# Adding the causal mask of the plain scores on VectorE, inside the maximum's instruction, instead of with a mask matmul

## What is computed

```python
score = jnp.einsum('bhqd,bhkd->bhqk', Q, K) / scale
causal = jnp.tril(jnp.ones((1, 1, seq, seq), dtype=jnp.float32))
score = score - 10000000000.0 * (1.0 - causal)
score = score - jnp.max(score, axis=-1, keepdims=True)
weights = jax.nn.softmax(score, axis=-1)
attn = jnp.einsum('bhqk,bhkd->bhqd', weights, V)
```

## Time and profile before

| | us |
|---|---|
| median of 3 runs | 498.72 |
| lowest, highest | 497.11, 499.74 |
| span of the profiled execution | 495.2 |
| busy: PE / PEld / DVE | 463.4 / 296.0 / 323.8 |
| busy: ACT / POOL | 285.1 / 166.9 |

### The profile page before, as it was taken

One profiled execution on the slowest core, in us unless ns is written; L12 is line 12 of the kernel. 1 busy time (PEld: TensorE's weight loads), 2 busy tenths in 40 slices (PEclk: granted clock), 3 DMA queues, 4 the chain that ended last, 5 costly groups with the idle time before them and its releaser, 6 DMA issues.

```text
span 495.2 us, 10480 instructions
## 1 busy us (share of the span) xinstructions
PE 463.4 (94%) x2676; PEld 296.0 (60%) x2676; DVE 323.8 (65%) x802; ACT 285.1 (58%) x594; POOL 166.9 (34%) x167
## 2 busy tenths in 40 slices
PE   5779999999999999999999999989999999999992
PEld 2346555555554654655655545447887787787781
DVE  3879757777677676777776774313656756756743
ACT  1311146765766766767657666956565565565560
POOL 4524010230411402402304112126645564564661
PEclk9986579999999999999999999999999999999997
DMA  7877411212112112202121000000000000000000
GB/s 249 267 226 192 122 21 26 68 33 66 40 19 64 40 19 64 57 18 67 37 65 39 3 1 3 2 0 1 1 1 3 21 0 0 21 0 0 22 0 22
DMA packets 41738, 23.49 MB, mean 47 GB/s; under 512 B 31280, under 2 KB 33968, under 8 KB 41712
## 3 DMA queue, kind: packets, MB, share of 16 engines
q1 hardware_dynamic: 41712, 23.18, 17.1%
HBM read 14.26 MB, written 8.65 MB: 46 GB/s over the span
## 4 chain that ended last, share of the span: by engine, by line
PE 77%; DVE 7%; issue 4%; ACT 4%; DMA 4%; SPq 3%; POOL 1%; DVEq 0%; ACTq 0%; POOLq 0%
PE bank L960 20%; PE bank L975 15%; PE bank L1044 14%; PE bank L938 14%; PE bank L1055 7%; DVE maxima L703 2%; PE bank L993 2%; DMA k_scratch<-rope_lo 2%; PE bank L941 2%; ACT num L600 1%; DVE num L763 1%; DVE num L836 1%; ACT num L539 1%; SPq L314 1%; PE bank L1020 1%
## 5 line engine op out<-in xcount | busy, mean ns | idle before, releaser
L539 ACT ACTIVATE num<-bank 128x512 f32<-128x512 f32 (+3 forms) x384 | 168.8, 495 | 101.6 <-PE bank L960 99.1
L703 DVE TENSOR_REDUCE maxima<-bank 128x1 f32<-128x512 f32 (+15 forms) x384 | 182.3, 519 | 66.9 <-PE bank L941 46.2
L960 PE MATMUL bank<-q_op,k_op 128*128 128x512 f32 (+3 forms) x384 | 148.2, 419 | 2.8 <-ACT num L539 1.7
L938 PE MATMUL bank<-k_op,q_op 128*128 128x512 f32 (+15 forms) x384 | 126.3, 369 | 3.4 <-issue 2.9
L437 POOL TENSOR_SCALAR_AFFINE_SELECT num<-num 128x512 f32<-128x512 f32 x64 | 40.6, 635 | 226.0 <-ACT num L539 224.1
L960 PEld LDWEIGHTS bank<-q_op,k_op 128*128 128x128 f32 x384 | 71.4, 197 | 69.1 <-ACT num L539 62.0
L468 POOL TENSOR_TENSOR q_op<-num,q_op 128x512 fp32r<-128x512 f32 x64 | 82.4, 1290 | 63.6 <-ACT q_op L593 60.3
L938 PEld LDWEIGHTS bank<-k_op,q_op 128*128 128x128 f32 x384 | 77.0, 202 | 19.2 <-DVE maxima L703 10.9
L1044 PE MATMUL bank<-q_op,w_hi 128*128 (+1 forms) x256 | 81.9, 401 | 1.7 <-DVE num L836 1.6
L975 PE MATMUL bank<-num,v_op 128*32 128x512 f32 (+3 forms) x768 | 82.5, 503 | 0.0
L836 DVE TENSOR_TENSOR num<-bank,num 128x512 f32<-128x512 f32 x64 | 44.2, 691 | 58.5 <-ACT num L600 54.8
(11 more groups left out here) (86 smaller groups left out, 315.7 us busy)
## 6 DMA issues: line engine op xcount, KB each, us to landing
k_op<-k_scratch SPq DMA_DIRECT2D x16, 256.0 KB, 2.7
q_op<-q_scratch SPq DMA_DIRECT2D x64, 52.0 KB
w_raw<-in_w_all SPq DMA_DIRECT2D x6, 512.0 KB, 4.3
q_scratch<-rope_hi SPq DMA_DIRECT2D x8, 256.0 KB, 3.1
k_scratch<-rope_hi SPq DMA_DIRECT2D x8, 256.0 KB, 3.6
xT<-in_x_feat SPq DMA_DIRECT2D x4, 256.0 KB, 6.1
k_scratch<-k_op SPq DMA_DIRECT2D x2, 512.0 KB, 6.2
q_scratch<-rope_lo SPq DMA_DIRECT2D x4, 256.0 KB, 3.9
```

The lines of the kernel that those rows point to most:

```text
L539: act.activation(num[:, t % PB, h, off:CH], t_bank[k % TB][:, off:CH], ACT.Exp, scale=scale)\
L703: dve.tensor_reduce(maxima[:, half, j:j + 1], s_bank[k % SB][:, 0:width], AX.X, ALU.max)\
L938: ins = pe.matmul(s_bank[k % SB][:, 0:width], q_op[u][:, j, :, :].rearrange("p h q -> p (h q)"), k_op[u][:, lo:lo + width], start=True, st ...
L960: pe.matmul(t_bank[k % TB][:, off:CH].rearrange("p (j q) -> p j q", q=QD), k_op[w][:, kt * P:(kt + 1) * P], q_op[w][:, c * NB + off // QD: ...
```

## The change

The mask matmul at L941 goes; every plain unit is one matmul. The mask tile becomes `causal`, 512 columns wide in the tile `resid`: DVE clears the first 480 columns at the start of the program, and SP, after waiting for that, loads the 32 columns of the mask behind them, in fp32. For a diagonal unit DVE issues `tensor_tensor_reduce`, which adds the unit's last `width` columns of `causal` to the scores, writes the sum to one of three SBUF tiles (nothing reads them) and takes the maximum. Units that are not diagonal keep `tensor_reduce`. Ahead of the new instruction stands `dve.sem_inc(dve_turn, 1)`. In the first unit DVE also waits for the mask's load. The bf16 copies, their two casts on ScalarE and PE's wait for them go.

```diff
@@ -33,6 +33,7 @@
 QROWS = 3 * DH + 2
 KROWS = 3 * DH
 MASKED = -1e30
+LOWEST = -3e38
 FT = F // P
 UNITS = E * FT
 
@@ -177,8 +178,6 @@
 
         cos_sb, sin_sb = sb("cos_sb", [P, S]), sb("sin_sb", [P, S])
         ident = sb("ident", [P, P])
-        mask_f = sb("mask_f", [P, QD])
-        ident_b, mask_b = sb("ident_b", [P, P], BF16), sb("mask_b", [P, QD], BF16)
         tri = sb("tri", [P, 2, E * E])
         wqk = sb("wqk", [P, 4, D])
         wv, wo = sb("wv", [P, D]), sb("wo", [P, D])
@@ -210,6 +209,7 @@
 
         mg_w, mg_t, x1_w, x1_tw = (sb(n, [P, CH]) for n in ("mg_w", "mg_t", "x1_w", "x1_tw"))
         resid = sb("resid", [P, CH])
+        causal, masked_s = resid, (mg_w, mg_t, x1_w)
         x1 = xT[:, :].rearrange("p (t d) -> p t d", d=D)
 
         flat = [q_op[u][:, :, :, :].rearrange("p j h q -> p (j h q)") for u in range(2)]
@@ -248,7 +248,7 @@
         max_split, small_ready, small_read = sem("max_split"), sem("small_ready"), sem("small_read")
         rows_loaded = [sem(f"rows_loaded{c}") for c in range(NC)]
         dve_step, dve_turn, pool_turn = sem("dve_step"), sem("dve_turn"), sem("pool_turn")
-        w_split, w_hi_done, small_cast = sem("w_split"), sem("w_hi_done"), sem("small_cast")
+        w_split, w_hi_done, causal_cleared = sem("w_split"), sem("w_hi_done"), sem("causal_cleared")
 
         c_mg, c_mgt, c_mgs, c_y, c_var, c_rstd, c_x1, c_x1t, c_hi, c_log, c_lo, c_tanh, c_store, c_top = (
             sem(n) for n in ("c_mg", "c_mgt", "c_mgs", "c_y", "c_var", "c_rstd", "c_x1", "c_x1t",
@@ -277,7 +277,8 @@
                     sp.dma_start(sin_sb[:, cols], sin_t[:, cols]).then_inc(ld_tab[ch], 16)
                 if ch == 0:
                     sp.dma_start(wv[:, :], vw).then_inc(ld_v, 16)
-            for dst, src in ((ident[:, :], ident_d), (mask_f[:, :], mask_d)):
+            sp.wait_ge(causal_cleared, 1)
+            for dst, src in ((ident[:, :], ident_d), (causal[:, CH - QD:CH], mask_d)):
                 sp.dma_start(dst, src).then_inc(ld_small, 16)
 
             sp.wait_ge(ops_filled, 1)
@@ -504,10 +505,6 @@
                                bank[3][:, :], ACT.Copy).then_inc(v_copied, 1)
 
             for n in range(2 * CHUNKS):
-                if n == 4:
-                    act.wait_ge(ld_small, 16 * 2)
-                    act.activation(ident_b[:, :], ident[:, :], ACT.Copy).then_inc(small_cast, 1)
-                    act.activation(mask_b[:, :], mask_f[:, :], ACT.Copy).then_inc(small_cast, 1)
                 if n in (PROJ_FIRST - 1, PROJ_FIRST + 1):
                     copy_v((n - PROJ_FIRST + 1) // 2)
                 act.wait_ge(roped_ready, n + 1)
@@ -642,6 +639,7 @@
             dve.sem_inc(f_lo, HB)
 
 
+            dve.memset(causal[:, 0:CH - QD], 0.0).then_inc(causal_cleared, 1)
             for u in range(2):
                 dve.memset(v_op[u][:, :, :, :], 0.0).then_inc(v_cleared, 1)
             dve.wait_ge(v_cleared, 2)
@@ -700,8 +698,16 @@
                         lo = half * CH
                         width = min(CH, QD * (j + 1) - lo)
                         dve.wait_ge(s_ready, NS * s + k + 1)
-                        dve.tensor_reduce(maxima[:, half, j:j + 1], s_bank[k % SB][:, 0:width], AX.X, ALU.max)\
-                            .then_inc(s_reduced, 1)
+                        if QD * (j + 1) - lo <= CH:
+                            if k == 0 and plan is PROLOGUE:
+                                dve.wait_ge(ld_small, 16 * 2)
+                            dve.sem_inc(dve_turn, 1)
+                            dve.tensor_tensor_reduce(masked_s[k % SB][:, 0:width], s_bank[k % SB][:, 0:width],
+                                                     causal[:, CH - width:CH], 1.0, LOWEST, ALU.add, ALU.max,
+                                                     maxima[:, half, j:j + 1]).then_inc(s_reduced, 1)
+                        else:
+                            dve.tensor_reduce(maxima[:, half, j:j + 1], s_bank[k % SB][:, 0:width], AX.X, ALU.max)\
+                                .then_inc(s_reduced, 1)
                         done += 1
                         if done == SEG_S[0]:
                             split_max(s, 0, chain)
@@ -910,7 +916,6 @@
                 if n == PROJ_FIRST - 2:
                     project_v(0)
             pe.wait_ge(ld_small, 16 * 2)
-            pe.wait_ge(small_cast, 2)
             pe.sem_inc(pv_done, PB)
 
             def stage(plan, s, u, turn_u, turn_v, small):
@@ -933,14 +938,9 @@
                         once(k_loaded[u][half], turn_u * 16, ("k", half))
                         lo = half * CH
                         width = min(CH, QD * (j + 1) - lo)
-                        diagonal = QD * (j + 1) - lo <= CH
                         pe.wait_ge(s_reduced, NS * s + k + 1)
-                        ins = pe.matmul(s_bank[k % SB][:, 0:width], q_op[u][:, j, :, :].rearrange("p h q -> p (h q)"),
-                                        k_op[u][:, lo:lo + width], start=True, stop=not diagonal)
-                        if diagonal:
-                            ins = pe.matmul(s_bank[k % SB][:, width - QD:width], ident_b[:, :], mask_b[:, :],
-                                            start=False, stop=True)
-                        ins.then_inc(s_ready, 1)
+                        pe.matmul(s_bank[k % SB][:, 0:width], q_op[u][:, j, :, :].rearrange("p h q -> p (h q)"),
+                                  k_op[u][:, lo:lo + width], start=True, stop=True).then_inc(s_ready, 1)
                     if step[0] == "P":
                         if step[1] + 1 < 2 * CHUNKS:
                             project(step[1] + 1)
```

## The result

| | before | after |
|---|---|---|
| median of the runs, us | 498.69 (497.11 to 499.74, 4 runs) | 503.56 (501.81 to 504.83, 4 runs) |
| span of the profiled execution, us | 495.2 | 500.0 |
| busy PE / DVE, us | 463.4 / 323.8 | 456.8 / 326.0 |
| DVE instructions recorded | 802 | 1059 |

The ratio is 1.0111, 95% interval 1.0069 to 1.0153: slower by more than the 0.5% that a measurement can tell. The forecast was 499.0 us, no change. The time lies outside the forecast's own case (496.3 to 501.4) and inside the whole range, between the forecast and rival A's 506.6, and that it does so is luck: the range was drawn from prices of the new instruction, and what made the time longer is something else.

What follows compares the result with a forecast made beforehand. TensorE seemed to set the pace (busy 94%), but which engine is late at each place decides. Seven steady stages gave -0.8 us, the first +1.1: +0.3 on 498.7 made 499.0 us, range 493.5 to 508.5.

Steps and rivals of the forecast that it cites:

- rival A: On VectorE the second instruction doesn't overlap the first, 0.16 us per masked unit: slower, 506.6 us, chance 0.35.
- What the addition costs: VectorE's added instructions and separate wait: +0.28 and +0.24 us in a steady stage, +1.1 us in the first stage.
- start, eight short units: At a stage's start, masked units at least 0.30 us apart make PE's fifth score wait: +0.24 us a stage.
- maxima chain: Units of 448, 480, 512 and 64 columns, around 208.5 to 213.6: four second instructions on the path, +0.28 us a stage.
- the steps that end at 217.5 and 220.9: Two steps of a steady stage, already chained to reductions: removing masks gains only 0.075 and 0.07 us.
- A mask inside a burst costs 0.12 us: On PE, between score matmuls: 0.04 us for the mask matmul itself, 0.08 for a weight load that nothing covers.
- The second instruction at 0.08 us per unit: On VectorE, the instruction that writes the maximum behind each masked unit's sum adds 0.08 us per unit.
- rival B: On VectorE the second instruction is nearly free, 0.02 us, and issue runs ahead: faster, 494.4 us, chance 0.26.
- The separate wait: A semaphore instruction between wait and reduction on VectorE: masked units at least 0.30 us apart, 0.08 more from data to start.
- The first stage, +1.1 us: Reductions run without a gap from about 44 to 57 us, so 14 masked units add 0.08 us each.
- C: The summing instruction runs at half rate on VectorE, 1.24 us for 512 columns: 524 us, chance 0.03.
- a stage over 34.5 says A: Sign: a steady stage over 34.5 us would show that the second instruction doesn't overlap the first; 33.8 was forecast.

Runs made afterwards that it cites:

- wait_apart: Before with VectorE looping over one stage, the wait for PE moved to a separate semaphore instruction ahead of each masked reduction: 500.28 us, ratio 1.0063.
- the padded kernels: Before with semaphore instructions added behind masked reductions, the wait left on the reduction, with VectorE's loop of two stages or of one: 498.05 to 508.58 us.
- before_short_loop: Before with VectorE's loop over one stage per iteration instead of two, a body of 122 instructions: 497.92 us, ratio 1.0014.
- before_padded_half: Before with the loop of two stages and one semaphore instruction added behind each masked reduction, a body of 306 instructions: 498.05 us, ratio 1.0023.
- before_padded_short: Before with two semaphore instructions added behind each masked reduction and VectorE looping over one stage, a body of 186: 499.51 us, ratio 1.0054.

## Why the prediction went wrong, point by point

**The step that failed** is not in the sum at all. "What the addition costs" priced each added instruction by its time on the engine and by its spacing, and asked nothing of the program that holds them. The order of the change showed the two rows per unit; their number in a loop body was there to be counted. It goes from 242 to 370, and each of two turns leaves DVE idle for 3.3 and 3.7 us at a place where three banks are full and nothing covers. The stages that end with a turn are 2.9 and 3.3 us longer than in the change with a shorter loop. The two behind them, in which PE runs at the lower clock for 3.5 us, are 0.8 and 0.7 us longer. That is 7.7 us. The first steady stage gives 1.2 back, for a reason of its own (last point below), and the spans differ by 7.0 (500.0 and 493.0). Without the stalls the change stands at 0.9976 of before, 497.5 us, within "no change" and 1.5 us under the forecast.

**The sum's own terms**, in us for a steady stage, change with the shorter loop against before with the shorter loop (medians of the steps between PVs):

| place | predicted | measured |
|---|---|---|
| start, eight short units | +0.24 | +0.39 |
| 384 columns and NORM, with a mask ahead of its PV | -0.15 | -0.10 |
| maxima chain (fourth and fifth step, -0.09 and +0.16) | +0.28 | +0.07 |
| the steps that end at 217.5 and 220.9 | -0.075, -0.07 | -0.17, -0.13 |
| two masks between 222 and 224 | -0.22 | -0.21 |
| two around 226 | -0.09 | -0.14 |
| mask ahead of a PV where PE paces | -0.03 | -0.04 |
| sum | -0.12 | -0.33 |

- **A mask inside a burst costs 0.12 us**: right. PE's timeline of after, where the same units of 320 and 512 columns follow each other:

```profile
228.71 0.31 PE L942 MATMUL bank<-k_op,q_op 128*128 128x320 f32 x1
228.86 0.40 PE L960 MATMUL bank<-q_op,k_op 128*128 128x512 f32 x1
229.10 0.39 PE L942 MATMUL bank<-k_op,q_op 128*128 128x512 f32 x1
```

From score to score 0.39 us, where before it was 0.51.

- **The second instruction at 0.08 us per unit**: wrong for long units, where it is nearly free, as rival B had it; for the short ones at a stage's start about right, by another mechanism (next point). DVE's timeline of after:

```profile
229.21 0.49 DVE L705 CUSTOM_DVE_ANT_0 x_w<-bank,resid 128x320 f32<-128x320 f32 x1 [0.77 <-PE bank L942]
229.63 0.08 DVE L705 DVE_READ_ACCUMULATOR2_ANT maxima<- 128x1 f32 x1
229.63 0.69 DVE L709 TENSOR_REDUCE maxima<-bank 128x1 f32<-128x512 f32 x1
```

The read starts 0.42 us after its unit, and the next reduction starts together with it. A plain reduction of 320 columns would give way after some 0.41 (0.61 for 512 columns, less 0.20 for 192 columns at the 0.53 for 512). So the read adds about 0.01 to the spacing, and its end, at 229.71, is 0.01 behind that of the unit. The rule of the Trainium skill that the next op cannot issue until the pipeline is empty (VectorE: DVE Perf Modes, § The DRAIN you can't avoid) does not hold for this pair; the same section says that a next op that is not held starts earlier, which this pair agrees with. The Trainium skill's rule that an accumulator output makes two instructions (VectorE: DVE Perf Modes, § Two Vector instructions with no wait between them) agrees with the trace.
- **The separate wait**: right in kind and too small. The prediction had 0.30 us as the least spacing in the loop; it is 0.34 (206.04, 206.39, 206.74). The two places were right and the causes of their prices weren't. At the start the price follows the number of instructions per unit, whichever they are (wait_apart and the padded kernels). In the fifth step +0.12 comes with the moved wait (wait_apart), and the chain as a whole cost +0.07 where +0.28 was put.
- **The first stage, +1.1 us**: 35.94 us against 34.69 in the two traces, +1.25; but the two kernels with the shorter loop have 35.56 and 35.33, +0.23. The two kernels without the change do the same in this stage and differ by 0.64 us, with a granted clock of 0.66 and 0.60 in it (0.64 in after, 0.61 in the change with the shorter loop). One execution each doesn't settle a term of 1.1 us, and it stays open.
- **The first steady stage** was priced like the others, -0.12. It is not like them. The stretches of before and, behind it, of the change with the shorter loop:

```profile
60.80:97.90 37.10, 36.80 (x237) 20.91 (x237) 25.19 (x59) 22.70 (x51) 5.42 (x9) 0.90 0.15 34
```

```profile
61.80:97.50 35.70, 34.83 (x204) 19.69 (x203) 25.52 (x93) 22.65 (x52) 5.92 (x10) 0.92 0.16 37
```

Here the granted clock is 0.90, and PE is busy for 36.8 of 37.1 us: with part of the stage at the lower level PE sets the pace, and the stage is 1.4 us shorter with the change. Not all of that is the change's. The lower level lasts until 68.0 us in before and until 67.5 in the change with the shorter loop, 7.2 and 5.9 us of the stage. After runs the same instructions here, with 3.7 us at the lower level, and takes 34.5 us, 1.2 less for 2.2 us less at that level. At this rate, an estimate from these two traces, 0.7 of the 1.4 us is the clock's and 0.7 the change's, several times the 0.12 that the prediction gave the stage.

**The rivals.** Rival A has the right side and is 3 us off, by a mechanism that isn't there: the read does overlap. Rival B has the right instruction in the long units and the wrong time. C falls: a unit of 512 columns takes 0.68 us, as the reduction does, and the 1.24 us of the earlier trace rows on which it rested is the mean of eight subtractions that took between 0.67 and 1.75. Of the signs named at the end, steady stages of 33.8 us came true only where the loop was shortened (33.9); "a stage over 34.5 says A" was met by after's stages of 34.7 and 34.6, and would have led to the wrong cause. What spoke against A was in the same trace: the pair's spacing, and 3.7 us of "issue" in one place, which no cost per unit can make.

## What to carry to other kernels

Where a change adds instructions to an engine's loop, count its body before and after, with its accumulator reads and with the register and semaphore instructions, which no profile row shows as busy; on VectorE here 306 were held and 338 were not. A program that is fetched again shows itself by "issue" ahead of the first instruction after the turn and by more instruction transfers on the page. Then halve the body or write it out: the same change went from 1.1% slower to the time of before (halved; 0.9976, within the noise) and to 1.2% faster (written out). Where TensorE waits out such a hole, look at its granted clock behind it too.

## What the runs showed of the hardware

- **A loop body of VectorE is held up to some length, then fetched anew at every iteration.** Instruction transfers of after between 125 and 275 us:

```profile
q14 instruction: 10, 0.08, 0.2%
```

Ten of 8 KB each: the trace has them start at 132.0, 134.4, 136.8, 159.3 and 182.1 us behind the first branch (130.7), and at 204.0, 206.4, 208.8, 231.4 and 253.9 behind the second (202.3), five per turn. In before none ran on that queue between 130 and 290 us. Bodies of 122, 186, 242 and 306 instructions gave no such wait, 338 and 370 gave 3.1 to 3.7 us at each turn. The Trainium skill (Runtime: NRT & Kernel Launch, § Instruction fetch mechanics) says that a taken branch to a target outside the current window forces a fetch before execution can go on; the traces agree. The same section of the Trainium skill gives the memory of such an engine as 512 instructions, refilled in blocks of 16 KiB. By the count alone 370 would have fitted, and the transfers here are of 8 KB; the runs put the limit for this body between 306 and 338.
- **A hole on VectorE lowers TensorE's clock behind it.** With PE busy 1.07 of 4 us, the granted clock was 0.53 in the 3.5 us from 206.50 (after); the stage took 0.7 us longer.
- **A wait on an instruction of its own** delays the start: the trace of after records the semaphore instruction at 210.81 us and the unit behind it at 210.96, 0.15 us later; in wait_apart the fifth step grew by 0.12.
- **Short instructions in a row are spaced by the number of instructions, those without data included:** from the first to the fifth unit of a stage 0.21 us apart in the mean with none added (before_short_loop), 0.24 with one (before_padded_half), 0.32 with two (before_padded_short).
- **The accumulator read** takes 0.08 us and runs beside the next instruction.
- **The summing maximum** of 512 columns, one operand in PSUM and one in SBUF, takes 0.68 us, as a plain reduction does (0.69).
